# A sum's place in TensorE's queue: four matmuls of the y sum ahead of a block's side jobs in a two-layer selective scan

## The chip, the cores and the metric

One core of one Trainium2 chip runs the whole program. The metric is the device time of one execution in microseconds (us). The kernel before takes 28649.85 us, the median of 3 runs (28649.08 to 28655.97).

## The reference

The input is 16 images of 48 x 48 positions with 96 channels. Two layers follow each other; each is a residual selective-scan block ("conv") and a residual feed-forward block of quantised products. What matters here is the scan in the middle of each conv block. Four directions `k` scan the 2304 positions of an image, with 192 inner channels and 16 states:

```
xc    = silu(depthwise_conv(xc))               # 192 channels, 48 x 48
xs    = [xc by rows, xc by columns, and both reversed]      # K = 4 directions
dts, Bm, Cm = split(x_proj(xs))                # 6, 16 and 16 rows for each direction
delta = softplus(dt_proj(dts) + bias)
h     = h * exp(delta_t * A) + (delta_t * u_t) * B_t        # for each of 2304 steps
y_t   = sum over the 16 states n of  h[n] * C_t[n]
y     = the four directions merged, + D * xs
```

`A` is negative and fixed, `u` is `xs`. Layer 0 gates `y` with silu(z) and has a convolution branch behind it; layer 1 normalises it first. Both end in the feed-forward block.

## The kernel before

**Stages.** A loop over 16 images stands inside a loop over the two layers. For each image there is a front (normalise, project, convolve, x projection), the scan, and a tail (gate or normalise, branch, feed-forward). The scan is about four fifths of an image's 895 us (28644.9 us for 32 passes).

**Groups and blocks.** The scan of an image is cut into 18 groups (`NG`, numbered 0 to 17 here) of 16 blocks (`NS`, numbered 0 to 15), one block for each of the 16 states. A group (`group(g)`, L70) is one pair of directions `p`, one tile of 128 channels `j` and one third `k` of the positions, 768 columns (`CH`). The tiles come in the order 1, 2, 0: groups 0 to 5 are tile 1, groups 6 to 11 tile 2, groups 12 to 17 tile 0. `it` counts the blocks, 288 for an image, 9216 for the program.

**What a block does**, engine by engine:

- ScalarE (ACT) computes `exp(A[n] * delta)` over 128 x 768 (L1066) into one of six state buffers (`NW`).
- TensorE (PE) brings the input term into one of two slots of PSUM. In a plain block (`broadcast`, L742, matmuls at L757) it spreads B over the partitions, and VectorE (DVE) multiplies the slot by `du = delta * u` (L1301). In a turned block (`turned`, L87, lines of `TURNED`, L83) ScalarE makes the product in transposed form (`scale_du`, L1107, activations at L1119) and TensorE transposes it back (`turn_product`, L734, L739), so that VectorE has no multiplication to do. Blocks 2, 4, 6, 9, 10, 13, 14 and 15 are turned in tiles 2 and 0, blocks 4, 6, 10, 13 and 14 in tile 1.
- VectorE runs the recurrence, one scan instruction over 768 columns (L1306).
- GpSimd (POOL) multiplies the state by C (`hC`, L1444) into one of four buffers (`NH`). It may write a buffer only when the y sum of four blocks ago has read it (semaphore `y_summed`, L1439).
- TensorE adds this product to the y sum in PSUM with the identity as weights (`add_state`, L761, four matmul instructions at L769). It does so `LAG` = 4 blocks later: in block `it` of TensorE's queue stands the sum of block `it - 4`, and it waits for GpSimd's product of that block (`hc_ready`). For the first block of a group it waits also until ScalarE has moved the last group's finished sums out (`emptied`, L781; `move_sums`, L1148, copy at L1154), or in layer 0's last three groups until VectorE has gated them (`gate_sums`, L1313).

A slot of PSUM comes free with the scan of two blocks ago (`scanned`), so TensorE can fill the slot for one block while VectorE scans the block before it.

**Side jobs.** The next group's `delta` and `du` are made meanwhile, by steps that `STEP_AT` (L111) puts at certain blocks. On TensorE they are: `pre_delta(g + 1)` at block 1 (L684, four matmuls at L702); `in_proj_z` at block 8 in groups 0 to 5 (L661), `merge_columns` at block 8 in groups 7 to 9 (L673, L679 and L680); `turn_b` at block 11 of groups 0 and 1 (L705); `turn_du(g + 1)` at block 15 (L717, six transposes at L731). All of them write the part `pre_part` of PSUM. On ScalarE: `keep_duT` copies the result of `turn_du` at block 1 of the group it is for (L1102, L1105), just before the first `scale_du`; then `move_sums` at block 5 (L1154), `evacuate` of the next group's `pre_delta` (L1025, L1032 and L1033), and the steps of softplus at blocks 5 to 7 (L1038, L1044, L1048, L1052); at block 11 of group 6 `gates` (L1138, L1141 and L1142). ScalarE's first task in each block is the exponential; it is allowed up to six blocks ahead of GpSimd's product (L1061). GpSimd has four steps of softplus at blocks 6, 7, 9 and 10.

**What sets the order.** There is no planner. Each engine has one queue, written out in its own `scan(g)` loop, and waits on semaphores in it; a waiting instruction holds everything behind it. On TensorE the order within a block is the slot's matmuls, then the block's side jobs, then the y sum of four blocks ago:

```python
if n == STEP_AT["du"] and g + 1 < NG:
    turn_du(g + 1)
if NS * g + n >= LAG:
    add_state(NS * g + n - LAG)
```

Of the kernel before, what the change touches and what calls it, by code (L numbers as in the profile page):

```python
# [30 lines left out]
DIN, NS, DR = 192, 16, 6  # L31
# [24 lines left out]
LAG = 4  # L56
# [13 lines left out]
def group(g):  # L70

    s, k = g // NC, g % NC
    p, j = tile_of(s)
    return s, p, j, k, (k if p == 0 else NC - 1 - k)
# [12 lines left out]
def turned(it):  # L87

    g = it // NS
    return g > 0 and it % NS in TURNED[group(g)[2]]  # L90
# [82 lines left out]
def metaformer(nc, x, wpacks, consts_f, consts_b, mid, c_rows, out):  # L173
    ctx = ExitStack()
    with ctx:
# [118 lines left out]
        def v(name, n):  # L294

            k = per(name, At.layer)
            base = 0 if At.layer == 0 else (NB + (name in AHEAD)) * per(name, 0)
            return At.image * k + (base + n)

        def wcol(name):  # L300
            at, n = COLS[At.layer][0][name]
            return wp[:, at:at + n]
# [91 lines left out]
        def by_column(a):  # L394
            return a.rearrange("p (c r) -> p r c", r=H)
# [167 lines left out]
        def _(pe):  # L563
# [50 lines left out]
            def c_rows_of(c):  # L614

                w = wcol("w_xb").rearrange("p (t m) -> p t m", t=3)
                if c == 0:
                    pe.wait_ge(sem["pre_taken"], v("pre_taken", 1))
                else:
                    pe.wait_ge(sem["c_copied"], v("c_copied", c))  # L620
                for h in range(2):
                    at = c * CH + h * SEG
                    for j in (0, 2, 1):
                        mm = pe.matmul(pre_part[0:NBC, h, :], w[:, j, :], u[j][:, at:at + SEG], start=(j == 0), stop=(j == 1))  # L624
                mm.then_inc(sem["c_ready"], 1)
# [35 lines left out]
            def in_proj_z(i):  # L661

                t, c = Z_UNITS[i]
                m = (P, DB)[t]
                pe.wait_ge(sem["pre_taken"], v("pre_taken", i + 2))
                hold(pe)
                for h in range(2):
                    at = c * CH + h * SEG
                    mm = pe.matmul(pre_part[0:m, h, :], wcol("w_in")[0:DM, (2 + t) * P:(2 + t) * P + m], xT[:, at:at + SEG],
                                   start=True, stop=True)  # L670
                mm.then_inc(sem["z_ready"], 1)

            def merge_columns(c):  # L673

                pe.wait_ge(sem["pre_taken"], v("pre_taken", FIRST_MERGE + c + 2))
                hold(pe)
                for h in range(2):
                    at, r = c * CH + h * SEG, (2 * c + h) * SEGROWS
                    pe.matmul(pre_part[0:DB, h, :], ident[:, 0:DB], u[1][:, at:at + SEG], start=True, stop=False)  # L679
                    mm = pe.matmul(pre_part[0:DB, h, :], ident[:, DB:P], by_column(u[1])[:, r:r + SEGROWS, :],  # L680
                                   start=False, stop=True)
                mm.then_inc(sem["merge_ready"], 1)

            def pre_delta(g):  # L684

                s, p, j, k, c = group(g)
                w = wcol("w_dt").rearrange("p (a t m) -> p a t m", a=PAIRS, t=3)
                if g == 0:
                    pe.wait_ge(sem["xa_copied"], v("xa_copied", 1))
                    hold(pe)  # L690
                else:
                    pe.wait_ge(sem["pre_taken"], v("pre_taken", g))
                    hold(pe)
                    if g == 1:
                        pe.wait_ge(sem["c_copied"], v("c_copied", NC))
                    if g > 1:
                        pe.wait_ge(sem["duT_ready"], v("duT_ready", g - 1))
                        hold(pe)
                rows = slice(DT_AT + 32 * p, DT_AT + 32 * p + 2 * DR)
                for h in range(2):  # L700
                    at = c * CH + h * SEG
                    mm = pe.matmul(pre_part[:, h, :], w[rows, p, j, :], xa[rows, at:at + SEG], start=True, stop=True)  # L702
                mm.then_inc(sem["pre_ready"], 1)
# [30 lines left out]
            def turn_product(it):  # L734

                pe.wait_ge(sem["scanned"], v("scanned", it - 1))
                pe.wait_ge(sem["prod_scaled"], v("prod_scaled", turned_before(it) + 1))
                for i in range(TBL):
                    mm = pe.transpose(slots[it % 2][:, i * P:(i + 1) * P], prod[turned_before(it) % 2][:, i * P:(i + 1) * P], ident)  # L739
                mm.then_inc(sem["b_bcast"], 1)  # L740

            def broadcast(g, n):  # L742

                s, p, j, k, c = group(g)
                it = NS * g + n
                if it < 2:
                    pe.wait_ge(sem["st_rest"], v("st_rest", it + 1))
                    pe.wait_ge(sem["st_moved0"], v("st_moved0", 16 * 6))
                    if it == 1:
                        pe.wait_ge(sem["xa_copied"], v("xa_copied", 2))  # L750
                else:
                    pe.wait_ge(sem["scanned"], v("scanned", it - 1))
                if g == 1 and n == 0:
                    pe.wait_ge(sem["st_moved1"], v("st_moved1", 16 * 6))
                at = n * (2 * P) + j * DB
                for a, m in ((0, BANK), (BANK, CH - BANK)):
                    mm = pe.matmul(slots[it % 2][:, a:a + m], sel[:, at:at + P], stacks[p][0:96, c * CH + a:c * CH + a + m],  # L757
                                   start=True, stop=True)
                mm.then_inc(sem["b_bcast"], 1)

            def add_state(it):  # L761

                g, n = it // NS, it % NS
                s, p, j, k, c = group(g)
                pe.wait_ge(sem["hc_ready"], v("hc_ready", it + 1))
                if n == 0 and g > 0:
                    emptied(g - 1)
                for h in range(2):
                    mm = pe.matmul(y_part[:, h, :], ident, hC[it % NH][:, h * SEG:(h + 1) * SEG], start=(n == 0), stop=(n == NS - 1))  # L769
                mm.then_inc(sem["y_summed"], 1)  # L770
                if p == 1 and n == 8:
                    for h in range(2):
                        at = c * CH + h * SEG
                        pe.matmul(y_part[:, h, :], ident, ysum[:, at:at + SEG], start=False, stop=False)  # L774
                        pe.matmul(y_part[:, h, :], diag_D[:, j, :], u[j][:, at:at + SEG], start=False, stop=False)  # L775
                if p == 1 and j == 0 and n == 10:
                    for h in range(2):
                        r = (2 * c + h) * SEGROWS
                        pe.matmul(y_part[:, h, :], ident, by_column(u[2])[:, r:r + SEGROWS, :], start=False, stop=False)  # L779

            def emptied(g):  # L781

                if At.layer == 0 and g >= NG - NC:
                    pe.wait_ge(sem["y_gated"], v("y_gated", g + 1 - (NG - NC)))
                else:
                    pe.wait_ge(sem["y_moved"], v("y_moved", g + 1))

            def scan(g):
                for n in range(NS):
                    if turned(NS * g + n):  # L790
                        turn_product(NS * g + n)
                    else:
                        broadcast(g, n)
                    if g == 0 and n + 1 < NC:
                        c_rows_of(n + 1)
                    if n == STEP_AT["pre"] and g + 1 < NG:
                        pre_delta(g + 1)
                    if n == STEP_AT["second"]:
                        if g < len(Z_UNITS):
                            in_proj_z(g)  # L800
                        if 0 <= g - FIRST_MERGE < NC:
                            merge_columns(g - FIRST_MERGE)
                    if n == STEP_AT["turn_b"] and g < PAIRS:
                        turn_b(g)
                    if n == STEP_AT["du"] and g + 1 < NG:
                        turn_du(g + 1)
                    if NS * g + n >= LAG:
                        add_state(NS * g + n - LAG)

            def last_sums():  # L810
                for it in range(NIT - LAG, NIT):
# [123 lines left out]
            def body(layer):  # L935
                front(layer)
                for g in range(NG):
                    scan(g)
                last_sums()
                tail(layer)  # L940
# [672 lines left out]
```

## Time and profile before

| | |
|---|---|
| runs | 28649.85 us median of 3 |
| profiled execution | 28646.71 us, its span 28644.9 us, mean granted TensorE clock 0.926 |
| PE, DVE busy | 88%, 87% of the span |
| ACT, POOL busy | 78%, 74% |
| y sum (L769) on PE | 36864 matmul instructions, 13702.3 us busy |
| scan instruction (L1306) on DVE | 9216, 16216.8 us busy |
| product with C (L1444) on POOL | 9216, 16554.6 us busy |

The profile is of one execution, taken on the core. PE stands for TensorE's matmuls and PEld for its weight loads, which overlap them; matmul ends are modelled, so that two groups that follow without a pause overlap by up to 0.3 us in the timeline, and the distance between two starts is the better measure. `[0.52 <-PE ps L757]` behind an instruction is the idle time of its engine before it and the instruction whose end released it. A line of a timeline can hold several instructions (`x6`). Front and tail of an image contain none of the lines that the change moves.

### The profile page before, as it was taken

What the parts mean: (1) busy time and instruction counts of PE and PEld (TensorE: products, weight loads), DVE (VectorE), ACT (ScalarE), POOL (GpSimd) and SP (SyncE); (2) the same over time, 40 slices, a digit from 0 to 9 for tenths busy, and PEclk for the clock granted to TensorE, in tenths of its full rate; (3) what the DMA queues carried; (4) which work ended last, traced back from release to release, by engine and by line L of the source; (5) the groups of instructions that cost most, each with busy time, mean ns of one, the idle gap of its engine ahead of it and who ended that gap; (6) DMA issues with size and microseconds to landing.
All of it is one profiled execution on the core that took longest, in us unless ns stands there. A gap on an engine that the chain in (4) does not pass through costs nothing.

```text
span 28644.9 us, 392408 instructions
## 1 busy us (share of the span) xinstructions
PE 25232.5 (88%) x98628; PEld 14578.7 (51%) x98628; DVE 24852.4 (87%) x17608; ACT 22384.5 (78%) x50661; POOL 21286.6 (74%) x12100
## 2 busy tenths in 40 slices
PE   8888988888888888889889998888998889988889
PEld 4445544455445544455445555555555555555555
DVE  8888998889888998889988898888898888988888
ACT  8777877778777887778777787777887777877778
POOL 8677876778767886778766787666786667876667
PEclk9898999999999998989989999999999999999999
DMA  4333443344333443334434354333443333444334
GB/s 152 116 119 120 155 129 118 119 129 157 118 118 118 141 146 117 119 120 155 130 112 128 128 160 134 125 127 127 142 154 126 126 128 128 158 136 126 128 127 140
DMA packets 1414970, 3764.29 MB, mean 131 GB/s; under 512 B 205408, under 2 KB 205536, under 8 KB 1412064
## 3 DMA queue, kind: packets, MB, share of 16 engines
q1 hardware_dynamic: 1412448, 3736.27, 40.7%
q8 instruction: 899, 14.73, 0.2%
q14 instruction: 1623, 13.30, 0.2%
HBM read 3659.95 MB, written 47.19 MB: 129 GB/s over the span
## 4 chain that ended last, share of the span: by engine, by line
PE 30%; issue 29%; DVE 22%; ACT 14%; POOL 4%; DMA 1%; DVEq 0%; ACTq 0%; SPq 0%; POOLq 0%
PE ps L769 12%; DVE ps L1301 8%; DVE arena L1306 7%; ACT arena L1119 6%; DVE arena L529 4%; PE ps L739 3%; ACT arena L1066 3%; POOL arena L1444 2%; PE ps L757 2%; PE ps L932 1%; PE ps L931 1%; PE ps L774 1%; PE ps L775 1%; PE ps L624 1%; PE ps L779 1%
## 5 line engine op out<-in xcount | busy, mean ns | idle before, releaser
L1444 POOL TENSOR_TENSOR arena<-arena 128x768 f32<-128x768 f32 x9216 | 16554.6, 1822 | 1960.9 <-DVE arena L1306 1471.4
L769 PE MATMUL ps<-arena,consts 128*128 128x384 f32 x36864 | 13702.3, 495 | 371.5 <-ACT arena L1154 210.2
L1306 DVE TENSOR_TENSOR_SCAN arena<-arena,carry,ps 128x768 f32<-128x768 f32 x6144 | 10913.1, 1805 | 416.8 <-PE ps L739 261.2
L1066 ACT ACTIVATE arena<-arena,An 128x768 f32<-128x768 f32 x9216 | 8447.5, 930 | 666.3 <-POOL arena L1444 652.6
L769 PEld LDWEIGHTS ps<-arena,consts 128*128 128x128 f32 x36864 | 6361.9, 192 | 4057.7 <-issue 405.2
L1306 DVE TENSOR_TENSOR_SCAN arena<-arena,ps 128x768 f32<-128x768 f32 x3072 | 5303.7, 1747 | 460.3 <-PE ps L739 275.6
L1301 DVE TENSOR_TENSOR ps<-ps,arena 128x768 f32<-128x768 f32 x5344 | 5042.9, 944 | 543.2 <-PE ps L757 538.4
L1119 ACT ACTIVATE arena<-arena 128x64 f32<-128x64 f32 (+1 forms) x14976 | 4267.1, 367 | 586.7 <-PE ps L739 564.9
L739 PE MATMUL ps<-consts,arena 128*128 128x128 f32 x23232 | 3277.3, 278 | 1062.4 <-DVE arena L1306 747.4
L739 PEld LDWEIGHTS ps<-consts,arena 128*128 128x128 f32 x23232 | 2672.0, 142 | 2816.7 <-issue 1661.3
L1119 ACT ACTIVATE arena<-arena,bT 128x64 f32<-128x64 f32 (+1 forms) x13056 | 3789.4, 372 | 89.5 <-PE ps L739 67.7
L757 PE MATMUL ps<-arena,consts_b 96*128 96x512 bf16 x10688 | 2676.8, 333 | 670.2 <-DVE arena L1306 512.4
L757 PEld LDWEIGHTS ps<-arena,consts_b 96*128 96x128 bf16 x10688 | 904.6, 99 | 2993.3 <-DVE arena L1306 1684.6
L1481 POOL MEMSET arena<- 128x100 f32 x112 | 21.2, 189 | 2964.3 <-DVE arena L1351 2797.5
L529 DVE SCALAR_TENSOR_TENSOR arena<-arena,wp 128x2304 f32<-128x2304 f32 (+2 forms) x896 | 2114.0, 2359 | 31.6
L1458 POOL TENSOR_TENSOR arena<-arena 64x1152 bf16<-64x1152 f32 x64 | 174.1, 2720 | 1777.3 <-ACT arena L1021 1777.3
L1130 ACT COPY carry<-arena 128x1 f32<-128x1 f32 x6144 | 1087.0, 177 | 213.9 <-DVE arena L1306 213.4
L1468 POOL TENSOR_TENSOR arena<-arena 128x768 f32<-128x768 f32 x544 | 992.1, 1824 | 0.0
L1477 POOL TENSOR_TENSOR arena<-arena 128x768 f32<-128x768 f32 x544 | 991.7, 1823 | 0.0
L547 POOL TENSOR_TENSOR arena<-arena 128x1920 f32<-128x1920 f32 x128 | 592.2, 4627 | 534.8 <-ACT arena L538 526.1
L1472 POOL TENSOR_TENSOR arena<-arena 128x768 f32<-128x768 f32 x544 | 989.5, 1819 | 0.0
L1463 POOL TENSOR_TENSOR arena<-arena 128x768 f32<-128x768 f32 x544 | 989.3, 1819 | 0.0
(172 smaller groups left out, 22107.1 us busy)
## 6 DMA issues: line engine op xcount, KB each, us to landing
arena<-c_rows SPq DMA_DIRECT2D x6144, 384.0 KB, 3.8
arena<-c_rows SPq DMA_DIRECT2D x6144, 192.0 KB, 3.5
arena<-arena SPq DMA_DIRECT2D x384, 72.0 KB, 2.0
c_rows<-arena SPq DMA_DIRECT2D x96, 192.0 KB, 3.5
arena<-x SPq DMA_DIRECT2D x17, 864.0 KB, 4.5
arena<-mid SPq DMA_DIRECT2D x17, 864.0 KB, 4.4
mid<-arena SPq DMA_DIRECT2D x16, 864.0 KB, 4.2
out<-arena SPq DMA_DIRECT2D x16, 864.0 KB, 4.1
```

What stands on the lines that cost most here:

```text
L529: i = dve.scalar_tensor_tensor(out=o, in0=src, scalar=w[:, tap:tap + 1], in1=o, op0=ALU.mult, op1=ALU.add)
L739: mm = pe.transpose(slots[it % 2][:, i * P:(i + 1) * P], prod[turned_before(it) % 2][:, i * P:(i + 1) * P], ident)
L757: mm = pe.matmul(slots[it % 2][:, a:a + m], sel[:, at:at + P], stacks[p][0:96, c * CH + a:c * CH + a + m], start=True, stop=True)
L769: mm = pe.matmul(y_part[:, h, :], ident, hC[it % NH][:, h * SEG:(h + 1) * SEG], start=(n == 0), stop=(n == NS - 1))
L1066: act.activation(state_at[it % NW], delta[g % 2], ACT.Exp, scale=An[:, slot(s) * NS + n:slot(s) * NS + n + 1]).then_inc(sem["da_ready"], 1)
L1119: last = act.activation(prod[q % 2][:, at], duT[g % 2][:, at], ACT.Copy, scale=bT[p][:, TBL * c + i, n, h:h + 1])
L1130: act.copy(carry[:, n:n + 1], state_at[it % NW][:, end:end + 1]).then_inc(sem["end_kept"], 1)
L1301: dve.tensor_tensor(slots[it % 2], slots[it % 2], du[g % 2], ALU.mult).then_inc(sem["dbu_ready"], 1)
L1306: dve.tensor_tensor_scan(a[:, ::back], a[:, ::back], slots[it % 2][:, ::back], 0.0 if k == 0 else carry[:, n:n + 1], ALU.mult, ALU.add).th ...
L1444: pool.tensor_tensor(hC[it % NH], state_at[it % NW], Csb[b], ALU.mult).then_inc(sem["hc_ready"], 1)
L1468: pool.tensor_tensor(e, spln, e, ALU.add).then_inc(sem["sp_log1p"], 1)
L1477: pool.tensor_tensor(du[g % 2], delta[g % 2], chunk(u[j], c), ALU.mult).then_inc(sem["du_ready"], 1)
```

## The change

In TensorE's `scan(g)` the call of `add_state` goes from the end of the block to the place behind the slot's matmuls (and, in group 0, behind `c_rows_of`), ahead of the block's side jobs. Nothing else is changed: the same instructions with the same waits, in another order in the blocks that have a side job. These are block 1 and block 15 in 17 groups, block 8 in 9 groups and block 11 in 2 groups of an image. In all other blocks the order stays.

```diff
                     if g == 0 and n + 1 < NC:
                         c_rows_of(n + 1)
+                    if NS * g + n >= LAG:
+                        add_state(NS * g + n - LAG)
                     if n == STEP_AT["pre"] and g + 1 < NG:
                         pre_delta(g + 1)
                     if n == STEP_AT["second"]:
...
                     if n == STEP_AT["du"] and g + 1 < NG:
                         turn_du(g + 1)
-                    if NS * g + n >= LAG:
-                        add_state(NS * g + n - LAG)
```

## Rows read from the trace of the kernel before

**Rows 1.** The page: busy time of the engines over the span, and the chain that ended last.
```profile
PE 25232.5 (88%) x98628; PEld 14578.7 (51%) x98628; DVE 24852.4 (87%) x17608; ACT 22384.5 (78%) x50661; POOL 21286.6 (74%) x12100
...
PE 30%; issue 29%; DVE 22%; ACT 14%; POOL 4%; DMA 1%; DVEq 0%; ACTq 0%; SPq 0%; POOLq 0%
```

**Rows 2.** Busy time of each engine in 200 us of an image's scan (stretch first, clock after POOL).
```profile
10400.00:10600.00 200.00, 186.86 (x773) 108.42 (x774) 186.02 (x129) 186.94 (x444) 186.73 (x105) 0.98 0.50 164
```

**Rows 3.** Waits, whole span: who waited for whom, total us, times, longest.
```profile
PEld ps L769 <- POOL arena L1444: 386.5, 541, 4.6
...
PEld ps L769 <- ACT arena L1154: 324.2, 480, 1.5
...
ACT arena L1105 <- PE ps L731: 250.8, 223, 2.4
...
POOL arena L1444 <- PE ps L769: 176.5, 135, 3.9
```

**Rows 4.** Timeline, block 15 of group 9 to block 5 of group 10, one image.
```profile
10525.09 0.82 PE L739 MATMUL ps<-consts,arena 128*128 128x128 f32 x6
...
10525.74 0.82 PE L731 MATMUL ps<-consts,arena 128*128 128x128 f32 x6
...
10526.40 1.46 PE L769 MATMUL ps<-arena,consts 128*128 128x384 f32 x4
10526.60 0.80 ACT L1105 COPY arena<-ps 128x768 f32<-128x768 f32 x1
...
10527.69 0.49 PE L757 MATMUL ps<-arena,consts_b 96*128 96x512 bf16 x2
...
10536.46 0.78 ACT L1154 COPY arena<-ps 128x768 f32<-128x768 f32 x1
...
10537.29 1.56 PE L769 MATMUL ps<-arena,consts 128*128 128x384 f32 x4 [0.30 <-ACT arena L1154]
...
10538.68 0.49 PE L757 MATMUL ps<-arena,consts_b 96*128 96x512 bf16 x2
...
10539.77 0.94 DVE L1301 TENSOR_TENSOR ps<-ps,arena 128x768 f32<-128x768 f32 x1
```

**Rows 5.** Timeline of ScalarE, then VectorE: group 6, its copy, block 12.
```profile
10371.20 0.80 ACT L1105 COPY arena<-ps 128x768 f32<-128x768 f32 x1 [0.21 <-PE ps L731]
...
10402.47 0.93 ACT L1066 ACTIVATE arena<-arena,An 128x768 f32<-128x768 f32 x1
...
10403.52 1.75 DVE L1306 TENSOR_TENSOR_SCAN arena<-arena,ps 128x768 f32<-128x768 f32 x1 [2.48 <-ACT arena L1066]
```

**Rows 6.** Timeline, block 15 of group 12 to block 5 of group 13, same image.
```profile
10632.71 0.82 PE L739 MATMUL ps<-consts,arena 128*128 128x128 f32 x6
...
10633.37 0.82 PE L731 MATMUL ps<-consts,arena 128*128 128x128 f32 x6
...
10634.78 1.56 PE L769 MATMUL ps<-arena,consts 128*128 128x384 f32 x4 [0.60 <-POOL arena L1444]
...
10634.84 0.94 ACT L1066 ACTIVATE arena<-arena,An 128x768 f32<-128x768 f32 x1 [1.03 <-POOL arena L1444]
10635.68 0.78 ACT L1105 COPY arena<-ps 128x768 f32<-128x768 f32 x1
10636.18 0.49 PE L757 MATMUL ps<-arena,consts_b 96*128 96x512 bf16 x2
...
10636.71 0.97 DVE L1301 TENSOR_TENSOR ps<-ps,arena 128x768 f32<-128x768 f32 x1 [1.19 <-PE ps L757]
...
10645.52 0.78 ACT L1154 COPY arena<-ps 128x768 f32<-128x768 f32 x1
...
10646.36 1.56 PE L769 MATMUL ps<-arena,consts 128*128 128x384 f32 x4 [0.71 <-ACT arena L1154]
...
10647.75 0.49 PE L757 MATMUL ps<-arena,consts_b 96*128 96x512 bf16 x2
...
10648.28 0.97 DVE L1301 TENSOR_TENSOR ps<-ps,arena 128x768 f32<-128x768 f32 x1
```

## The prediction

> **What bounds the kernel now.** I read the page first: TensorE and VectorE are busy 88% and 87% of the span, ScalarE 78%, and no engine holds more than 30% of the chain that ended last [rows 1]. So no single engine sets the end. The busy time inside a scan says more: of 200 us ScalarE is busy 186.94, TensorE 186.86 and VectorE 186.02, at a granted clock of 0.98 [rows 2], the upper level (2.4 GHz) nearly throughout. ScalarE, which the page shows with a fifth of its time free, has 13 us in 200 here. Next the waits: TensorE's y sum waited 386.5 us for GpSimd's products and 324.2 us, in 480 places (15 of an image's 18 groups), for ScalarE's copy of the finished sums; ScalarE waited 250.8 us for `turn_du`; GpSimd waited for the y sum only 176.5 us [rows 3]. Last come timelines of group boundaries, since the change touches blocks 15 and 1 in nearly every group. There the reader is to look for what stands right behind `turn_du` on ScalarE, and how far that work is ahead of VectorE five blocks later.
>
> **The change, part by part.** It adds and removes no instruction, no DMA and no wait. In 45 blocks of an image's 288 it exchanges a side job with a y sum. TensorE's own work stays the same: in a boundary without a wait the starts are 0.65 us (transposes of block 15), 0.66 (`turn_du`) and 1.29 (y sum) apart [rows 4], and a sum of three terms doesn't depend on their order. What changes is who is served when: the y sum comes 0.66 us or more earlier, the side job 1.29 us later.
>
> *(1) Block 15, regular groups.* In group 9's block 15 `turn_du` starts at 10525.74, ends at 10526.56, and ScalarE's copy for group 10 starts at 10526.60 [rows 4]: nothing lies between. With the y sum first, `turn_du` starts at 10527.03 and the copy can't start before 10527.89, 1.29 us late. Behind the copy ScalarE has scalings, exponentials and the copy of the finished sums (L1154) at 10536.46; in the whole timeline of that stretch I found no pause of over 0.2 us, so that copy slips by 1.29 as well. TensorE already waits for it (0.30 us, then the matmul at 10537.29 [rows 4]), so the first y sum of the group and the slot behind it slip too: that slot's matmuls end at 10538.68 + 0.49 = 10539.17, and VectorE takes them at 10539.77. With 0.04 us from end to start the slack is 0.56 us; the other 0.73 us stop VectorE. This pattern is in groups 8 to 12 of all 32 passes, with slacks around this one, and in groups 16 and 17 of layer 1's 16 passes (in layer 0 VectorE gates the sums there, and ScalarE isn't asked). That is 5 x 32 + 2 x 16 = 192 times 0.73 = **140 us**. The bounds are 0, if the lag were made up, and 1.29 x 192 = 248 us, if there were no slack. Nothing gives it back later in the group, since TensorE waits for VectorE's slots again in the blocks that follow.
>
> *(2) Block 15 of groups 12, 13 and 14.* Here GpSimd is late: the y sum waits and starts at 10634.78, and `turn_du`, at 10633.37, has used the waiting time [rows 6]. With the y sum first, everything behind it on TensorE is held: `turn_du` starts 1.40 us (10636.18 less 10634.78) behind the y sum, at 10636.18, where the next broadcast stood, and the broadcast 0.65 us later. VectorE was already waiting 1.19 us for that broadcast [rows 6], so the 0.65 is lost in full. The copy starts at 10636.18 + 0.82 + 0.04 = 10637.04 in place of 10635.68, 1.36 late, of which VectorE's shift covers 0.65. Five blocks on, the slot's matmuls end at 10647.75 + 0.49 = 10648.24 and VectorE starts at 10648.28 [rows 6]: no slack, so the other 0.71 is lost as well. 1.36 x 3 x 32 = **131 us**; the bounds are 62 (the 0.65 alone) and 192 (0.65 and a whole 1.36).
> The Trainium skill ("TensorE: Matmul & The Clock Gate", Part 1, on the array's detail) says that TensorE's queue may pull weight loads ahead of matmuls in flight, while matmuls stay strictly in order. By the second half the 0.65 stands; by the first, one of the six loads could be done in the wait, and the sum would be some 10 us less (96 times a sixth of 0.65). The trace doesn't show which.
>
> *(3) Group 6.* The copy waits for `turn_du` (0.21 us), so it is late by the whole 1.29. Before block 12 ScalarE does the two long silu activations, and there VectorE waits 2.48 us for the exponential at 10402.47 [rows 5]. ScalarE is the bound there, and its lag shows nearly whole: 1.2 x 32 = **38 us** (bounds 0 and 41).
>
> *(4) The small ones.* In groups 10 and 11 the product for the y sum comes just as block 15's transposes end, and in groups 4 and 7 the copy has part of the slack of (1). I take 0.8 us an image, **26 us**, from nothing nearer than the terms above; bounds 0 and 70 (1.29 and the like in the two groups, less the overlap).
>
> *(5) Groups 1, 2, 3 and 5* belong to tile 1, whose first turned block is 4, not 2. ScalarE has a pause before it and takes the lag there: nothing; if that cover is gone, 0.73 x 128 = 93 us.
>
> *(6) Blocks 1, 8 and 11.* `pre_delta` ends 1.29 later, and its reader stands on ScalarE behind the copy at 10536.46, nearly nine us after block 0's matmuls at 10527.69 [rows 4]. The results of block 8 are read at blocks 11 and 12, those of block 11 at block 13. I cost all three at nothing, covered by two to four blocks; were the cover gone in blocks 8 and 11, it would be 1.29 x (9 + 2) x 32 = 454 us. The y sum that comes earlier could give back at most what GpSimd waits for it, 176.5 us [rows 3]; I take nothing of it, because at the boundaries above the slots, not GpSimd's buffers, hold VectorE. SyncE's and GpSimd's own queues keep their order, and their waits are for `hc_ready` and `y_summed`, neither of which comes later except by the shift itself.
>
> **Sum:** 140 + 131 + 38 + 26 = 335 us. The profiled execution took 28646.71 us, 3 us under the median of the runs shown, which changes nothing here: 28647 + 335 = 28982, so I forecast **28980 us**, 1.2% slower.
>
> **The rivals.**
> *ScalarE's lag is hidden, only TensorE's lost filler counts.* For it: the exponentials run blocks ahead. Against it: 480 waits for the copy of the sums [rows 3]. Then 62 us of (2) and a few of (4): 28715. The Trainium skill ("Perfetto Trace Analysis", on the most-contended engine) ranks VectorE, ScalarE and GpSimd by their share of busy time; by that ScalarE, at 78%, would be the last to look at, and the answer this rival's. Rows 2 disagree. Chance 0.12.
> *Faster.* Block 15's y sum frees GpSimd's buffer 0.66 us sooner, GpSimd's products come sooner, and with them the exponential that ScalarE takes just before the copy (it waited 1.03 us for GpSimd in rows 6). It decides if GpSimd waits for TensorE at most boundaries and the copy isn't bound by `turn_du`. All of the 176.5 us back would be 28470. The count of those waits, 135 in 9216 blocks, speaks against it. Chance 0.05.
> *Nothing moves*, lag and filler both covered: 28650, chance 0.05.
> *ScalarE is saturated.* If its lag is never made up within a group, (1) costs 248, (2) 192, (3) and (4) 70 to 110 us: about 29190. Rows 2 speak for it, the 0.56 us of slack in rows 4 against it. Chance 0.13.
> *The forecast*: 0.65.
>
> **How the numbers follow.** The forecast's own spread, from the bounds of (1) and (2), is about 28850 to 29090. Up to the first rival at 28715 or the last at 29190 the range would leave out too little; 28780 to 29110 leaves out the cases at 28715 and below (0.22) less what of the first comes with a part of the lag, and half of the last: about 0.2. A measurement of this kernel tells about 0.2% (57 us) from no change. Slower takes the forecast, the saturated case and most of the hidden one: 0.88. Same 0.07, faster 0.05.
>
> **What the changed profile would show.** ScalarE's waits for `turn_du` grow from 250.8 us to some 700 to 900, at over 400 places; TensorE's waits of L769 for L1154 grow by some 200 us; L769's for GpSimd grow; VectorE's waits for L757 grow most, at blocks 0 and 5. The clock stays. The forecast is wrong if the copy L1105 slips and L1154 doesn't, if L1154 slips and VectorE's start at block 5 doesn't, or if blocks 8 and 11 show waits that aren't there now.

## The result, and the profile after

After the change the kernel takes 29077.22 us (median of 4 runs, 29076.37 to 29079.76), before it 28649.47 us (4 runs, 28648.29 to 28655.97): the ratio is 1.0149, with a 95% interval of 1.0133 to 1.0165. It is 428 us slower. The sign is the one forecast, and the time lies in the range, 97 us above the 28980 that was named.

From here on "the block-15 part" is the exchange of the y sum with `turn_du`; starts are compared as distances from the first scan of the same group.

The page of the profile after, busy time and then the chain, answers to [rows 1]:

```profile
PE 25247.4 (87%) x98628; PEld 14651.2 (50%) x98628; DVE 24887.5 (86%) x17608; ACT 22374.8 (77%) x50661; POOL 21303.1 (73%) x12100
...
PE 32%; issue 23%; ACT 22%; DVE 16%; POOL 4%; DMA 1%; ACTq 0%; DVEq 0%; SPq 0%; POOLq 0%
```

The busy times are those of before within 0.5%; only the span grew. ScalarE's share of the chain went from 14% to 22%. The same 200 us of the same image (its group 6 starts its first scan at 10521.63 here and 10374.34 before, so the stretch is moved by 147.29) answer to [rows 2]:

```profile
10547.29:10747.29 200.00, 181.20 (x742) 104.88 (x742) 181.38 (x126) 183.40 (x435) 181.61 (x103) 0.98 0.49 162
```

Each of the four engines does 3.5 to 5.7 us less in the same time: no engine works longer, they wait for each other. The waits show for whom, answering to [rows 3] with three rows more:

```profile
ACT arena L1105 <- PE ps L731: 950.7, 544, 3.7
DVE ps L1301 <- PE ps L757: 852.9, 772, 4.7
PEld ps L769 <- ACT arena L1154: 749.4, 480, 2.3
...
POOL arena L1444 <- PE ps L769: 406.6, 494, 4.0
...
PEld ps L769 <- POOL arena L1444: 307.0, 290, 4.6
...
PE ps L769 <- POOL arena L1444: 91.9, 97, 1.3
```

The chain of the forecast is there link by link. ScalarE now waits for `turn_du` in every one of the 544 boundaries. TensorE waits for the copied sums in as many places as before (480), but 425.2 us longer. VectorE waits for the broadcast 314.5 us longer (538.4 before).

The timeline of the boundary of group 10 in that image answers to [rows 4]:

```profile
10676.99 1.46 PE L769 MATMUL ps<-arena,consts 128*128 128x384 f32 x4
...
10678.29 0.82 PE L731 MATMUL ps<-consts,arena 128*128 128x128 f32 x6
10678.94 0.49 PE L757 MATMUL ps<-arena,consts_b 96*128 96x512 bf16 x2
10679.14 0.80 ACT L1105 COPY arena<-ps 128x768 f32<-128x768 f32 x1 [1.22 <-PE ps L731]
...
10680.47 1.81 DVE L1306 TENSOR_TENSOR_SCAN arena<-arena,carry,ps 128x768 f32<-128x768 f32 x1
...
10689.01 0.77 ACT L1154 COPY arena<-ps 128x768 f32<-128x768 f32 x1
...
10689.83 1.56 PE L769 MATMUL ps<-arena,consts 128*128 128x384 f32 x4 [1.63 <-ACT arena L1154]
10691.23 0.49 PE L757 MATMUL ps<-arena,consts_b 96*128 96x512 bf16 x2
...
10691.75 0.97 DVE L1301 TENSOR_TENSOR ps<-ps,arena 128x768 f32<-128x768 f32 x1 [0.65 <-PE ps L757]
```

Counted from the group's first scan, the copy L1105 starts 1.29 us later than before (1.33 ahead of the scan in place of 2.62, the scan of before being at 10529.22), the copy of the sums 1.30 later (8.54 behind it, before 7.24), the y sum 1.29 later. TensorE's wait grew from 0.30 to 1.63, and VectorE, which hadn't waited there, stands 0.65 us.

The boundary of group 13 answers to [rows 6]:

```profile
10788.67 1.56 PE L769 MATMUL ps<-arena,consts 128*128 128x384 f32 x4 [1.23 <-POOL arena L1444]
...
10790.07 0.82 PE L731 MATMUL ps<-consts,arena 128*128 128x128 f32 x6
10790.72 0.49 PE L757 MATMUL ps<-arena,consts_b 96*128 96x512 bf16 x2
10790.92 0.80 ACT L1105 COPY arena<-ps 128x768 f32<-128x768 f32 x1 [1.26 <-PE ps L731]
...
10791.25 0.97 DVE L1301 TENSOR_TENSOR ps<-ps,arena 128x768 f32<-128x768 f32 x1 [1.82 <-PE ps L757]
```

The wait for GpSimd, of which `turn_du` had filled 0.65 us and left 0.60, is now 1.23 long in one piece; `turn_du` stands 1.40 behind the y sum, the broadcast 0.65 behind that, and VectorE's wait went from 1.19 to 1.82.

Group 6, blocks 12 to 14, answers to [rows 5]. Before, the scans waited 2.48, 1.51 and 1.36 us; blocks 13 and 14 were:

```profile
10405.20 1.54 PE L739 MATMUL ps<-consts,arena 128*128 128x128 f32 x6 [5.42 <-ACT arena L1119]
...
10409.04 0.82 PE L739 MATMUL ps<-consts,arena 128*128 128x128 f32 x6
...
10409.90 1.75 DVE L1306 TENSOR_TENSOR_SCAN arena<-arena,ps 128x768 f32<-128x768 f32 x1 [1.36 <-PE ps L739]
```

Now:

```profile
10551.88 1.75 DVE L1306 TENSOR_TENSOR_SCAN arena<-arena,ps 128x768 f32<-128x768 f32 x1 [3.28 <-ACT arena L1066]
...
10553.57 1.54 PE L739 MATMUL ps<-consts,arena 128*128 128x128 f32 x6 [5.98 <-ACT arena L1119]
10554.90 2.77 PE L769 MATMUL ps<-arena,consts 128*128 128x384 f32 x4
10555.15 1.75 DVE L1306 TENSOR_TENSOR_SCAN arena<-arena,ps 128x768 f32<-128x768 f32 x1 [1.51 <-PE ps L739]
...
10557.46 1.42 PE L739 MATMUL ps<-consts,arena 128*128 128x128 f32 x6
10558.72 1.46 PE L769 MATMUL ps<-arena,consts 128*128 128x384 f32 x4
...
10558.92 1.75 DVE L1306 TENSOR_TENSOR_SCAN arena<-arena,ps 128x768 f32<-128x768 f32 x1 [2.02 <-PE ps L739]
```

Here is something that the forecast doesn't have. ScalarE's lag gives 0.80 us at block 12. The 0.66 at block 14 comes from somewhere else: the transposes L739 in front of it took 1.42 us, where before they took 0.82. TensorE had waited 5.98 us (5.42 before). The granted clock was at the lower level behind the wait in both traces; counted from the scan of block 12, it was back at the upper level after 5.45 us before the change and after 6.81 now. Block 14's transposes start 5.52 us behind that scan before, just past the low stretch, and 5.58 now, inside it. Over the 32 passes group 6 spends 218 us at the lower level, before 137.

The same stands at group 17 of layer 1. First its timeline before the change, then after:

```profile
18880.88 1.56 PE L769 MATMUL ps<-arena,consts 128*128 128x384 f32 x4 [0.75 <-ACT arena L1154]
18882.27 0.49 PE L757 MATMUL ps<-arena,consts_b 96*128 96x512 bf16 x2
18882.60 1.46 PE L769 MATMUL ps<-arena,consts 128*128 128x384 f32 x4
```

```profile
19159.69 2.39 PE L769 MATMUL ps<-arena,consts 128*128 128x384 f32 x4 [2.04 <-ACT arena L1154]
19161.87 0.85 PE L757 MATMUL ps<-arena,consts_b 96*128 96x512 bf16 x2
19162.51 2.04 PE L769 MATMUL ps<-arena,consts 128*128 128x384 f32 x4
...
19164.39 0.82 PE L739 MATMUL ps<-consts,arena 128*128 128x128 f32 x6
19165.04 1.46 PE L769 MATMUL ps<-arena,consts 128*128 128x384 f32 x4
```

The granted clock around it (stretches; the clock is the number before the last two), after:

```profile
19150.00:19160.00 10.00, 7.42 (x32) 3.95 (x31) 9.89 (x8) 9.99 (x27) 7.52 (x5) 1.00 0.54 176
19160.00:19162.00 2.00, 2.00 (x5) 0.81 (x4) 1.06 (x1) 2.00 (x3) 1.25 (x1) 0.57 0.54 189
19162.00:19170.00 8.00, 7.74 (x29) 4.22 (x27) 7.17 (x6) 6.94 (x17) 5.41 (x3) 0.89 0.42 139
```

In the matching 30 us of before the clock is 1.00 throughout. With the longer wait (2.04 us in place of 0.75) TensorE fell from 2.4 to 1.2 GHz, and the next two y sums and the broadcast between them ran slow. VectorE stands 1.70 us for that broadcast.

To see where the 428 us are, I took the distance from each of the 9216 scans to the next in both traces. The distances within the images hold 423 us of the difference, in these groups (my own working from the two traces: after less before, us for one image, the step to the next group's first scan counted with the group before; group 0 has .24 and -.27, groups 1, 2, 3 and 5 have 0):

```
group            4     6     7    8    9    10   11   12    13    14    15   16   17
layer 0         .87  1.78  .49  .69  .93  .98  .89  1.43  1.37  1.32  .75  .72  .74
layer 1        -.02  2.16  .32  .69  .93  .99  .89  1.44  1.37  1.31  .79  .76  1.87
```

Groups 8 to 15 are almost the forecast's: 0.66 to 0.78 at block 5 of each (0.73 on average), and 0.65 more at the end of groups 12, 13 and 14. What is too much is in groups 6 and 17, and in places of layer 0 (4, 16, 17) where nothing or less was expected.

The traces' records of the granted clock say the same by themselves. Within the scans TensorE spends 623 us at the lower level before the change and 853 after, and the added 231 us (all 32 passes) lie in group 6 (82), group 17 of layer 1 (55), groups 16, 4 and 17 of layer 0 (51, 24 and 24), with -5 elsewhere. Groups 8 to 15, whose loss is the forecast's, have no time at the lower level in either trace. So two theories go into the experiments. **Theory A:** the forecast's terms hold, and the surplus is TensorE's clock, which falls in the longer waits. **Theory B:** the surplus is more lag of ScalarE, or another of the moved jobs (blocks 1, 8, 11).

### The profile page after: what moved, and what is told of

Read it like the earlier page. It is cut to its first block, busy times and chain, and to the rows that moved or that the text cites. A ratio compares the mean times of both kernels' runs of the same rounds, so it can differ in the third digit from the quotient of the medians.

```text
span 29074.9 us, 392408 instructions
## 1 busy us (share of the span) xinstructions
PE 25247.4 (87%) x98628; PEld 14651.2 (50%) x98628; DVE 24887.5 (86%) x17608; ACT 22374.8 (77%) x50661; POOL 21303.1 (73%) x12100
## 4 chain that ended last, share of the span: by engine, by line
PE 32%; issue 23%; ACT 22%; DVE 16%; POOL 4%; DMA 1%; ACTq 0%; DVEq 0%; SPq 0%; POOLq 0%
PE ps L769 14%; ACT arena L1119 10%; ACT arena L1066 5%; DVE arena L1306 5%; DVE ps L1301 5%; PE ps L739 4%; DVE arena L529 4%; POOL arena L1444 2%; PE ps L757 2%; PE ps L932 1%; PE ps L931 1%; PE ps L775 1%; PE ps L774 1%; PE ps L624 1%; PE ps L731 1%
## 5 line engine op out<-in xcount | busy, mean ns | idle before, releaser
L769 PEld LDWEIGHTS ps<-arena,consts 128*128 128x128 f32 x36864 | 6371.1, 193 | 4243.0 <-ACT arena L1154 749.4
L739 PE MATMUL ps<-consts,arena 128*128 128x128 f32 x23232 | 3317.6, 280 | 1062.8 <-DVE arena L1306 609.3
L739 PEld LDWEIGHTS ps<-consts,arena 128*128 128x128 f32 x23232 | 2666.6, 143 | 2981.9 <-issue 1648.5
L757 PE MATMUL ps<-arena,consts_b 96*128 96x512 bf16 x10688 | 2680.7, 333 | 607.8 <-DVE arena L1306 457.0
L757 PEld LDWEIGHTS ps<-arena,consts_b 96*128 96x128 bf16 x10688 | 932.6, 99 | 2669.8 <-DVE arena L1306 1472.7
L1105 ACT COPY arena<-ps 128x768 f32<-128x768 f32 x544 | 434.3, 798 | 950.7 <-PE ps L731 950.7
```

## The experiments

**Which block.** Each kernel makes the exchange only in some blocks, by a condition in TensorE's `scan(g)`:

```diff
+            def sum_first(g, n):
+                return n == STEP_AT["du"]
...
+                    if NS * g + n >= LAG and sum_first(g, n):
+                        add_state(NS * g + n - LAG)
...
-                    if NS * g + n >= LAG:
+                    if NS * g + n >= LAG and not sum_first(g, n):
                         add_state(NS * g + n - LAG)
```

Block 15 alone:

> The y sum goes ahead of the side job in block 15 only; blocks 1, 8 and 11 keep the order of before. If all of the loss comes from turn_du being late, the time is that of the changed kernel, 29077 (29060 to 29095). If the side jobs of blocks 1, 8 and 11 have a share in it, it is clearly lower, under 29020; if they had given something back, clearly higher, over 29120.

Measured 29079.52 us, ratio 1.0150 (1.0135 to 1.0166).

All the others, `n != STEP_AT["du"]`, that is blocks 1, 8 and 11:

> The complement: the y sum goes first in blocks 1, 8 and 11 only. The theory (their results are read two to four blocks later, and the earlier y sum frees nothing that anyone waits for) expects the time of before, 28650, within 30 us. The rival, that the earlier y sum feeds GpSimd, would give up to 176 us less, 28470 to 28600; a late side job that shows would give over 28700.

Measured 28644.42 us, ratio 0.9999 (0.9990 to 1.0008). The whole loss is block 15, and the other moved steps of an image cost nothing. There are 27 of them, not 28, and 44 exchanges in all: block 1 of group 0 has a side job but no y sum yet, since the sums start at block 4.

Block 15 of groups 12, 13 and 14 alone, `n == STEP_AT["du"] and g in (12, 13, 14)`:

> The y sum goes first in block 15 of groups 12, 13 and 14 only, where it waits for GpSimd. The forecast's price for these, 1.36 us each (0.65 of lost filler, 0.71 of ScalarE's lag), is 131 us: 28780 (28765 to 28800). With the filler alone it would be 62 us, 28712; with ScalarE's lag never made up 192 us, 28842.

Measured 28765.53 us, ratio 1.0043 (1.0027 to 1.0058), so 119 us. Its trace has the two parts in their places: 0.66 us at the end of each of the three groups, and 0.71, 0.66 and 0.78 at block 5 of groups 13, 14 and 15, together 4.1 x 32 = 132 us; the difference of -13 to the measured 119 is spread, with both signs, over groups 0, 4, 6, 7, 16 and 17 and the time between the images.

Block 15 of all the other groups, `g not in (12, 13, 14)`:

> The complement of the three groups: the y sum goes first in block 15 of all groups but 12, 13 and 14. If the parts add up, it costs what the whole (433 us) costs less what the three groups cost (119 us): 314 us, 28960 (28940 to 28980). If one delay hid behind the other, the sum of the parts is larger than the whole, and this is over 28990.

Measured 28913.53 us (28898 to 28930), ratio 1.0094 (1.0077 to 1.0110): 262 us, under the range. The two halves make 381 us, not 428. In groups 7 to 15 the halves add up (127 + 156 against 281 us by the scans). By the scans 62 us are missing in all, and they lie mainly in groups 0 (27), 4 (19) and 17 (16), where a plain lag would add. The clock doesn't: beside the kernel before, the two halves spend 17 us less and 146 us more at the lower level within the scans, the whole change 231 more. The 27 us of group 0 stand at its first scans, ahead of all that the change moves in an image, so they aren't the exchange's own work.

**ScalarE's lag alone.** TensorE's order stays as before, and ScalarE gets 1.28 us of idle work (the load of a function table that is in place already) right behind the copy L1105:

```diff
                 act.copy(duT[g % 2], ps[:, PRE_AT:PRE_AT + CH]).then_inc(sem["duT_ready"], 1)
+                nc.scalar.preload_act_table_set("natural_log_exp_and_others")
```

> Before, with one load of ScalarE's activation table (1.28 us in the trace) right behind the copy L1105 in all 17 groups, TensorE's order untouched: ScalarE's lag alone, with no late turn_du and no lost filler. If the lag is what costs, the groups lose what they lose in the changed kernel less the 0.65 us at three block boundaries, and some more in groups 7 and 13 to 15, whose copy had room before: 29050 (28980 to 29100). If ScalarE runs far enough ahead to hide 1.28 us, and the loss was TensorE's order, 28650 to 28680.

Measured 29001.84 us (28991 to 29047), ratio 1.0122 (1.0107 to 1.0138). The groups of ScalarE's instructions by line, then the waits:

```profile
L1106 ACT ACT_TABLE_LOAD x544 | 698.0, 1283 | 9.8
```

```profile
PEld ps L769 <- ACT arena L1155: 758.7, 482, 2.2
```

With the order of TensorE untouched, 355 us are lost (400 in the profiled execution, the slowest of its four), and TensorE's wait for the copied sums becomes 758.7 us, about the 749.4 of after (L1155 is the copy of the sums, one line down). The lag of ScalarE by itself makes most of the cost, the clock's part in it included: within the scans this trace has 911 us at the lower level. At the ends of groups 12 to 14 nothing is lost here: that 0.65 is TensorE's own. Groups 8 to 12 show 0.57 to 0.78 us at block 5, where after has 0.66 to 0.78. Group 13 of layer 0 loses 2.73 us there, and the clock shows why: its first y sum takes 2.72 to 2.84 us in all 16 images, and the group has 55 us at the lower level, where before and after have none.

**The five blocks of cover.** If ScalarE's lag reaches TensorE through the copy of the sums at block 5, moving that copy to block 4 should shorten the way and cost some of the slack, with the order of before and with that of after (`sums=5` becomes `sums=4` in `STEP_AT`):

> Before, with ScalarE's copy of the finished sums (L1154) at block 4 in place of 5. The sums are ready only at the end of TensorE's block 3 (about 36.3 in the timeline of group 10, where ScalarE would arrive at 34.7), so ScalarE waits some 1.7 us there and TensorE gets the copy no earlier. If ScalarE's lead over VectorE is what bounds a group, the 1.7 us come out at its smallest lead, blocks 9 to 12: some 6 to 7 us an image, 28860 (28780 to 28920). If ScalarE has time to spare behind block 5, nothing: 28650.

Measured 29334.78 us, ratio 1.0238 (1.0221 to 1.0255).

> The changed kernel with the same step at block 4. The stop of VectorE at block 5 (0.7 us in ten groups) goes, since ScalarE reaches the sums 1.7 us sooner than now; what is left is ScalarE's lag at blocks 9 to 12, the same as in the kernel before with this step, and the 0.65 us at three boundaries: 28940 (28880 to 29000), clearly under the changed kernel's 29077. If it isn't the copy of the sums through which the late turn_du reaches VectorE, 29077 or over.

Measured 29324.19 us, ratio 1.0235 (1.0218 to 1.0253). Both expectations missed by about 400 us. The timeline of the first, group 10, ScalarE's copy and VectorE's scan two blocks later:

```profile
10767.52 0.80 ACT L1154 COPY arena<-ps 128x768 f32<-128x768 f32 x1 [2.49 <-PE ps L769]
...
10774.47 1.81 DVE L1306 TENSOR_TENSOR_SCAN arena<-arena,carry,ps 128x768 f32<-128x768 f32 x1 [0.76 <-ACT arena L1066]
```

I had counted with a wait of 1.7 us and with an even lead of ScalarE over VectorE. The sums aren't finished when ScalarE comes to them at block 4, it stands 2.49 us, and VectorE waits for the exponential two blocks later, at block 6. In groups 10 to 15 more is lost at blocks 10 and 13; over the whole kernel VectorE's waits for the exponential grow from 119.5 to 404.5 us and those for the transposes L739 from 536.8 to 852.7. So this pair can't say whether the copy of the sums is the way by which the lag reaches TensorE. What it does show is that the two kernels can't be told apart: 11 us are 0.04%, well inside either interval. At blocks 5 and 6 of groups 8 to 12 their scans are within 0.05 us of each other, where without the moved copy the change costs 0.66 to 0.78. Once ScalarE has to wait at block 4 for the y sums anyway, a `turn_du` that is 1.29 us late costs nothing there. At the ends of groups 12 to 14 the exchange still costs up to 0.43 us, and other blocks give that back; that I can't explain.

**The clock.** TensorE gets idle matmuls (identity by identity, into columns of `pre_part` that nobody reads) in the waits where theory A sees the clock fall:

```diff
+            def keep_busy(g, n):
+                count = {(0, 6, 13): 22, (1, 6, 13): 22, (0, 16, 0): 10, (0, 17, 0): 16}.get((At.layer, g, n), 0)
...
+                for i in range(count):
+                    pe.matmul(ps[:, PRE_AT + 7 * P:PRE_AT + 8 * P], ident, ident, start=True, stop=True)
...
                 if n == 0 and g > 0:
+                    keep_busy(g, 0)
                     emptied(g - 1)
```

A first version, on the kernel after, put 20, 28 and 14 of them before the first y sum of groups 16 and 17 in layer 0 and 17 in layer 1:

> The changed kernel with idle matmuls (identity times identity into columns of PSUM that nobody reads, 14 to 28 of 128 columns) where TensorE waits before the first y sum of groups 16 and 17 in layer 0 and 17 in layer 1. There four matmuls take 2.4 to 2.9 us after the wait, against 1.46 elsewhere. If the loss beyond the forecast is the clock that falls in these waits, they take 1.5 us and the kernel wins 60 to 95 us: 29000 (28980 to 29020). If the matmuls are long for another reason (the bank, the copy's end), the fill changes nothing or costs: 29070 to 29100.

Measured 29076.18 us, ratio 1.0148 (1.0131 to 1.0165): no gain. The timeline (L772 is the idle matmul, L783 the y sum) says why:

```profile
10920.85 6.36 PE L772 MATMUL ps<-consts 128*128 128x128 f32 x40 [2.52 <-ACT arena L1047]
...
10927.05 1.46 PE L783 MATMUL ps<-arena,consts 128*128 128x384 f32 x4
...
19161.83 3.29 PE L772 MATMUL ps<-consts 128*128 128x128 f32 x28
...
19164.96 1.46 PE L783 MATMUL ps<-arena,consts 128*128 128x384 f32 x4
```

One idle matmul leaves two records, and 14 of them took 3.29 us, 0.235 us each; I had counted half. So the fillers were longer than the waits: group 16 of layer 0 lost 2.4 us an image by them, and the two groups 17 won 0.64 and 0.38. But the y sum behind each takes 1.46 us again, where it had taken 2.9, 2.9 and 2.4. The last two kernels have fillers cut to the waits, on the kernel before with the numbers of the diff above, and on the kernel after with `{(0, 6, 13): 24, (1, 6, 13): 24, (0, 17, 0): 18, (1, 17, 0): 8}`:

> Before, with idle matmuls sized to the waits (0.23 us each as the last fill showed): 22 in front of block 13's transposes of group 6 in both layers, 10 and 16 in front of the first y sum of groups 16 and 17 in layer 0. If the clock falls in these waits and comes back only after the next two or three jobs, group 6 gains some 1.5 us an image and the other two 1.3 us each in layer 0: 28550 to 28600, 0.2 to 0.35% under before. If a longer matmul behind a wait has another cause, 28650 or over.

Measured 28588.72 us (28579.67 to 28592.53), ratio 0.9979 (0.9970 to 0.9988), as expected.

> The changed kernel with the same, sized to its longer waits: 24 in group 6, 18 in group 17 of layer 0, 8 in group 17 of layer 1 (group 16 has none, as ScalarE's reads of that bank end too late). Gains of 1.7, 2.1 and 1.1 us: 28970 (28950 to 29000). The distance to before with its own fill stays the regular part of the loss, 390 to 420 us. If the fill gives nothing here, 29077 or over.

Measured 28931.17 us, ratio 1.0098 (1.0082 to 1.0113): under the range, and so is the distance to the filled kernel of before, which was to be 390 to 420 us. Group 17 of layer 1 in this kernel (L744 idle, L783 y sum, L770 broadcast) beside the two fences of that place above:

```profile
19051.88 1.95 PE L744 MATMUL ps<-consts 128*128 128x128 f32 x16
19054.09 1.56 PE L783 MATMUL ps<-arena,consts 128*128 128x384 f32 x4 [0.26 <-ACT arena L1168]
19055.48 0.49 PE L770 MATMUL ps<-arena,consts_b 96*128 96x512 bf16 x2
19055.81 1.45 PE L783 MATMUL ps<-arena,consts 128*128 128x384 f32 x4
```

The y sum starts 9.27 us behind the group's first scan (at 19044.82) in both kernels (19150.42 in the one after), so the copy is as late as it was; only the clock is different. The fillers take 146 us from the kernel after and 59 from the one before. Within the scans the time at the lower level falls to 406 and 388 us, from 853 and 623; groups 6 and 17 have none in either filled trace. Between the two filled kernels the change costs **342 us** (28931.17 less 28588.72), and by the scans:

```
group            0     4     6     7    8    9    10   11   12    13    14    15   16   17
layer 0        -.63   .33  1.06  .23  .69  .93  .99  .90  1.43  1.35  1.31  .79  1.38   .00
layer 1        -.42  -.07  1.06  .22  .69  .93  1.00 .90  1.43  1.37  1.31  .79   .76   .67
```

Group 17 of layer 1 fell from 1.87 to 0.67, group 6 from 1.78 and 2.16 to 1.06, group 17 of layer 0 from 0.74 to nothing, which is what the forecast says of it. Group 16 of layer 0 has a filler in one of the two kernels only (0 against 55 us at the lower level), and its 1.38 isn't the change's alone. Theory A holds for groups 6 and 17. Theory B falls: the other blocks cost nothing, and the lag is the same in filled and unfilled kernels.

The filled kernel with the order of before, 28588.72 us, is faster than both kernels of this case.

## Why the prediction was right, and what it missed

**Block 15, regular groups (term 1).** Forecast 0.73 us each, with a copy 1.29 late and 0.56 of slack. Measured between the filled kernels: 0.66, 0.78, 0.76, 0.66, 0.78 at block 5 of groups 8 to 12 in both layers, and 0.76 and 0.67 in groups 16 and 17 of layer 1. The mean is 0.73. The copies slip as forecast, and the idle 1.28 us on ScalarE gave nearly the same.

**Groups 12 to 14 (term 2).** Forecast 0.65 + 0.71 each. Measured 0.65 and 0.72 (0.71, 0.66, 0.78). The bound from the Trainium skill ("TensorE: Matmul & The Clock Gate", Part 1, on the array's detail), by which a weight load might be done early inside the wait, isn't seen: the loss is a whole 0.65, as by the second half of that rule, the strict order of matmuls, which the page has in its Part 2.

**Group 6 (term 3).** Forecast 1.2, measured 1.06 with the clock held (0.80 at block 12 and 0.26 at block 5), and 1.78 to 2.16 without.

**The small ones (term 4).** Forecast 0.8 us an image. Measured between the filled kernels: 0.23 at the ends of groups 10 and 11 each, 0.22 to 0.27 in group 7 and 0.15 in group 9, and 0.13 on average in group 4, together 1.0. No row stood behind the 0.8, so that it came near is luck.

**Groups 1, 2, 3, 5 and blocks 1, 8, 11 (terms 5 and 6).** Forecast nothing. The scans of groups 1, 2, 3 and 5 are unmoved, and the kernel with the other blocks alone is 0.9999 of before.

So the sum of 335 us is what the change costs where the clock is mostly held (342; by the scans without group 0 and group 16 of layer 0 it is 337). The forecast's spread of 28850 to 29090 was narrower than its bounds: those of terms 1 and 2 alone give 28773 to 29151. The step that failed is the sentence "The clock stays": the forecast put the clock at nothing. What that left out is about 86 us (428 less 342), of which the scans hold 80. The mean granted clock went only from 0.926 to 0.922, but the fall comes at the worst moment, right behind a wait, where everybody stands waiting for TensorE.

By the fillers' gains, after less before, the most is group 6 (29 us: 1.03 + 1.18 in the two layers against 0.31 + 0.09, times 16), group 17 of layer 1 (19) and group 17 of layer 0 (12); group 16 of layer 0 takes 11 off, as only the kernel of before has a filler there. These 49 us are what the fillers show. The other 31 are in groups 0, 4 and 7, which have no filler. Half of them, 16 us, are in group 0, at its first scans, and so not the exchange's work: their clock differs from trace to trace. In group 4 of layer 0 the first y sum is slow (over 2 us) in 8 images before and in 15 after, in layer 1 in 5 and 3, which matches that group's 0.87 and -0.02 us. But in the filled kernel of before, where nothing near group 4 was touched, it is slow in 2 images of layer 0 and in all 16 of layer 1, so that no more than the clock's part in it is shown. Group 7 has no time at the lower level in any of the four traces; I take its 6 us for what group 6 passes on to it, which isn't shown.

The Trainium skill ("TensorE: Matmul & The Clock Gate", "HAM oscillation — how this bites in real kernels") says that TensorE's clock can fall and rise again within a kernel, in its case where the matmuls stand waiting for a DMA. This trace shows it for a wait for another engine (0.57 of full speed behind the wait of 2.04 us for ScalarE). The kernel before had it too, at 85 us of lower level in group 17 of layer 0, so the forecast could have priced it.

**The things foretold.** ScalarE's waits for `turn_du` were to be 700 to 900 us at over 400 places; they are 950.7 at 544. TensorE's wait for L1154 was to grow by some 200; it grew by 425. The 200 was wrong arithmetic beside the forecast's own terms: TensorE's wait at the copy of the sums grew by 1.1 to 1.3 us in groups 6 and 8 to 12 (0.30 to 1.63 at group 10) and by 0.9 to 1.0 in groups 13 to 15, and only VectorE is spared the slack. Of VectorE's waits those for L757 grew most, as said (314.5). The weight loads' waits for GpSimd were to grow and fell from 386.5 to 307.0: in groups 12 to 14 the wait grew (the matmuls' own from 26.5 to 91.9), but in other places it shrank; that GpSimd catches up there while the rest stand still is my reading, not shown.

**The rivals.** That ScalarE's lag is hidden (28715) fell with the table loads: 355 us by lag alone. By its share of busy time, as the Trainium skill ("Perfetto Trace Analysis", on the most-contended engine) ranks these engines, one would look at VectorE (87%) first and at ScalarE (78%) second; the prediction called ScalarE the last, but GpSimd has 74%. The chain after, with ScalarE at 22%, and that run say that ScalarE's time counts all the same. That ScalarE is saturated (29190) comes nearest to the measured time after the forecast, but not by its mechanism: block 5 loses 0.66 to 0.78 us of a lag of 1.29, so the slack is there in every one of these groups. The gain from GpSimd's earlier buffers doesn't appear: its waits for the y sum grew from 176.5 to 406.6, as at group 10, where the y sum behind the late one is what it waits for.

## What to carry to other kernels

In a queue that runs in order, a side job whose result starts a chain on a full engine goes first, and the work that nobody waits for goes behind it. Busy shares over the span don't show which engine is full. Inside the stage they come closer, but here they don't decide it either: the four engines were busy 186.02 to 186.94 of 200 us. So measure the slack where the late result finally meets the engine that sets the pace. And when a change makes TensorE wait longer, add the price of its clock: look up what its next instructions cost behind a long wait in the same trace.

## What the runs showed of the hardware

TensorE's clock falls inside a busy scan. Behind a wait of 2.04 us the y sum took 2.39 us, the broadcast 0.85 and the next y sum 2.04, in place of 1.56, 0.49 and 1.46, and the granted clock was 0.57 for 2 us. Behind waits of 1.63 us in groups 10 and 13 the y sum took 1.56, the price at the upper level. The length of the wait doesn't decide it alone: in the kernel after, the first y sum of group 4, behind waits of 1.1 us, took over 2 us in 18 of 32 images. In the kernel with the table loads that of group 13, behind waits of 1.91 to 1.93, took 2.72 to 2.84 us in all images of layer 0 and 1.56 in 11 of 16 of layer 1.

Idle matmuls in such a wait give something back where the wait is there anyway: in the kernel before 55 us by the scans of groups 6, 16 and 17 ((0.31 + 0.09 + 1.49 + 1.57) x 16), and 59 by the medians. (All scans of that trace together hold only 28: groups 0, 4 and 7, with no filler, lost 27.) They take about 0.24 us each at the upper level. The first version, whose fillers outlasted the waits, gave nothing (29076.18 us against 28931.17).

The clock makes costs that don't add. Two halves of one change cost 119 and 262 us alone and 428 together. None of what is missing is in groups 7 to 15, where the halves add up, and the time at the lower level doesn't add either: 17 us less and 146 more for the halves, 231 more for the whole.
